# Graph layer with a mixture of experts on one core: ScalarE's 32 row transfers of each round go into the row buffer one round ahead, and one copy places all 128 rows

## The chip, the core and the metric

The kernel runs on one core of one Trainium2 chip. The metric is the device time of the whole program in microseconds (us), the median of several runs. A difference of about 0.2% is what a measurement of this kernel can tell from no change.

## The reference, cut to what matters

A graph of 6250 nodes with 256 features each and 200000 edges goes through one graph convolution, a mixture of 64 experts (two for each node), a normalisation over the nodes and a layer norm. The part that the change touches is the sum over the edges:

```python
deg_out = jnp.clip(jax.ops.segment_sum(ones, src, num_segments=n), 1.0)
deg_in = jnp.clip(jax.ops.segment_sum(ones, dst, num_segments=n), 1.0)
h = feats * jax.lax.rsqrt(deg_out)[:, None]
m = jax.ops.segment_sum(h[src], dst, num_segments=n) * jax.lax.rsqrt(deg_in)[:, None]
x = (m @ W_gc + b_gc) + (feats @ W_res + b_res)
```

`dst` is sorted, and it is drawn as 6250 * u**2. So the first nodes have many edges each and the last ones few: the kernel works on tiles of 128 nodes, and the first tile alone has a seventh of all edges, while the last tiles have some 2000 each.

## The kernel before, in words

First the kernel counts the edges of each source, scales the node features, and writes them to `table` in HBM. Then comes the edge stage, which is where the change lies. The edges stand in 1563 chunks of 128. Eight chunks make a group (1024 edges), six groups make a round: 196 groups, rounds 0 to 31 of six groups (q = 0 to 5), and a last round 32 of four. Group g is q = g % 6 of round g // 6. Each q has its own slot in a ring of six (`ring(q)`; slots 0 to 2 are shown as `ring`, slots 3 to 5 as `stage`).

- **GpSimd (POOL)** gathers a chunk with one indirect DMA (L516), 128 rows of 1 KB each. Before a group it waits for its indices (`idx_ready`) and until the slot is free (`acc_added`, L513). It takes all eight chunks of a group, but of the last slot (q = 5, `ROW_Q`) only seven. The eighth chunk of q = 5 comes row by row from two other queues, 128 single transfers of 1 KB for each of rounds 0 to 31.
- **SyncE (SP)** takes 96 of these rows. It loads the list of 128 sources (`list_rows`, L411, signal `listed`), reads the list into registers and issues 96 transfers into `row_buf`, which has two halves that alternate by round (L420). When they are there, it signals `rows_there` (L423). It works ahead: for round n it starts once round n - 2 was placed (`rows_placed`) and its list was read (`list_read`).
- **ScalarE (ACT)** takes the other 32 rows in four turns of eight (`fetch_rows`, L695), straight into the ring slot, after the steps q = 0 to 3 of the same round. Since it writes the slot itself, it first waits that the round before is added up (`acc_added >= it * RING`). After the fourth turn it copies SP's 96 rows from `row_buf` into the slot (`place_rows`, L702).
- In each step q ACT also writes the indices of the group six ahead (`indices`, L638), for which it waits that the group q of this round has been gathered, and then does its part of a **tick** if there is one.
- **VectorE (DVE)** makes a one-hot matrix for each group (L925; for group g it may start once the matmuls of group g - 2 are done, and it is next in line after the tick of the group before), a second one where a group reaches into another tile (L936), and adds the sums to `acc` (L1048).
- **TensorE (PE)** multiplies the one-hot matrices with the gathered rows (L1258, eight matmuls shown as x16). Before a group it waits for the gather, for the one-hot matrix, and for q = 5 also for `rows_placed` and for ACT's own 32 rows (`act_rows`).

A **tick** is the work on a tile of nodes that has all its edges: ACT copies the tile (L642, and L644 once the group is added), PE transposes and projects it, DVE adds and picks the experts, ACT writes the root (L665 to L671). It goes back and forth between the three engines. There are 49, one for each tile, and in the last rounds there is one for every second group.

After the last group POOL clears its buffers (L527, which waits for `acc_added` of all groups), and the expert stage follows: tables of slots, gathers, two matmuls for each of 64 experts, then the two normalisations.

Names: `step` is ACT's round, `ACT_TURNS` is 4, `SP_ROWS` 96, `par` the parity of the round. On ACT all rounds but 0 and 32 are one hardware loop.

Of the kernel before, what the change touches and what calls it, by code (L numbers as in the profile page):

```python
# [10 lines left out]
ACT = mybir.ActivationFunctionType  # L11
# [3 lines left out]
P = 128  # L15
N, D, EDGES = 6250, 256, 200000
# [8 lines left out]
CPG = 8  # L25
COLS = EB * P
GCOLS = COLS // CPG
RING = 6
HOTS = 2
GROUPS = -(-EDGES // (P * CPG))  # L30
STEPS = -(-GROUPS // RING)
# [6 lines left out]
ROW_Q = RING - 1  # L38
BLOCK = 32
SP_ROWS = 96  # L40
ACT_ROWS = 8
ACT_TURNS = (P - SP_ROWS) // ACT_ROWS
MAIN = 3
TG = 7
NB = NT // TG
# [17 lines left out]
def graph_moe_kernel(nc, x, src, dst, W_gc, b_gc, W_res, b_res, Wg, bg, w1, b1, w2, b2, gamma, beta, out):  # L63
    ctx = ExitStack()
    with ctx:
        def sb(name, shape, dt=F32):
            return ctx.enter_context(nc.sbuf_tensor(name, shape, dt))

        def sem(name):
            return ctx.enter_context(nc.semaphore(name))  # L70
# [55 lines left out]
        row_buf = sb("row_buf", [P, 2, D])  # L126
# [49 lines left out]
        def piece(n):  # L176
            taken_to[0] += n
            return arena[:, taken_to[0] - n:taken_to[0]]

        xg_pair = piece(2 * MAIN * D).rearrange("p (b k d) -> p b k d", b=2, k=MAIN)  # L180
        x30 = 4 * DK * H + 2 * D
        xg = [xg_pair[:, 0, :, :], xg_pair[:, 1, :, :],
              stage[:, x30:x30 + MAIN * D].rearrange("p (k d) -> p k d", k=MAIN)]
        AHEAD = len(xg)
        xgT = piece(MAIN * D).rearrange("p (k c r) -> p k c r", k=MAIN, c=DK)
        h1 = piece(MAIN * H).rearrange("p (k j r) -> p k j r", k=MAIN, j=HK)
        outs = piece(2 * MAIN * D).rearrange("p (b k d) -> p b k d", b=2, k=MAIN)
        xgx = piece(D)
# [40 lines left out]
        ha_ready, table_first, table_rest = sem("ha_ready"), sem("table_first"), sem("table_rest")  # L229
# [4 lines left out]
        rows_there, rows_placed, act_rows = sem("rows_there"), sem("rows_placed"), sem("act_rows")  # L234
        idx_ready = sem("idx_ready")
        gath = [sem(f"gath{q}") for q in range(RING)]
        hot_ready, group_mm, acc_added = sem("hot_ready"), sem("group_mm"), sem("acc_added")
# [12 lines left out]
        w1_in, w2_in, b2_in = ([sem(f"{w}_in{par}") for par in range(2)] for w in ("w1", "w2", "b2"))  # L250
        gathered = [[sem(f"gathered{b}{k}") for k in range(MAIN)] for b in range(AHEAD)]
        scattered = [[sem(f"scattered{par}{k}") for k in range(MAIN)] for par in range(2)]
# [31 lines left out]
        def ring(q):  # L284

            return ring_low[:, q, :, :] if q < RING // 2 else ring_high[:, q - RING // 2, :, :]

        def row_of(eng, reg):

            node = nc.s_assert_within(eng.snap(reg), 0, N - 1,  # L290
                                      skip_runtime_bounds_check_because="the list of sources holds nodes")
            return table[bass.ds(node, 1), :]
# [304 lines left out]
        def _(act):  # L597
# [82 lines left out]

            row_regs = [act.alloc_register(f"act_row{r}") for r in range(ACT_ROWS)]

            def fetch_rows(it, par, turn, first):
                r0 = SP_ROWS + turn * ACT_ROWS
                if turn == 0:
                    if first:
                        act.wait_ge(table_first, 16)
                        act.wait_ge(table_rest, 16 * (NB - 1))
                    else:
                        act.wait_ge(acc_added, it * RING)  # L690
                    act.wait_ge(listed, it * 16 + 16)
                    act.sem_inc(act_starts, 1)
                act.load(row_regs, row_list[0:1, bass.ds(par, 1), r0:r0 + ACT_ROWS])
                for r in range(ACT_ROWS):
                    act.dma_start(ring(ROW_Q)[r0 + r:r0 + r + 1, CPG - 1, 0:D], row_of(act, row_regs[r])).then_inc(act_rows, 16)  # L695
                if turn == ACT_TURNS - 1:
                    act.sem_inc(list_read, 1)

            def place_rows(it, par):
                act.wait_ge(rows_there, it + 1)  # L700
                act.sem_inc(act_starts, 1)
                act.activation(ring(ROW_Q)[0:SP_ROWS, CPG - 1, 0:D], row_buf[0:SP_ROWS, bass.ds(par, 1), :],  # L702
                               ACT.Copy).then_inc(rows_placed, 1)

            def step(it, first):
                par = 0 if first else nc.s_assert_within(act.snap(it & 1), 0, 1,
                                                         skip_runtime_bounds_check_because="it is a parity")
                for q in range(RING):
                    ahead = q + LEAD
                    indices(it + ahead // RING, ahead % RING, first and ahead < RING)  # L710
                    group_ticks(it * RING + q)
                    if q < ACT_TURNS:
                        fetch_rows(it, par, q, first)
                    if q == ACT_TURNS - 1:
                        place_rows(it, par)
            step(0, True)
            with act.Fori(1, STEPS - 1) as it:
                step(it, False)
            it = STEPS - 1
            for q in range(LASTQ):  # L720
                group_ticks(it * RING + q)
# [486 lines left out]
        def _(pe):  # L1208
# [114 lines left out]
            def step(it, first, final=False):  # L1323
                for q in range(LASTQ if final else RING):
                    g = it * RING + q
                    c = group_code(pe, g)
                    first_tile, last_tile = field(pe, c, 0), field(pe, c, 1)
                    n = LASTJ if final and q == LASTQ - 1 else CPG
                    pe.wait_ge(gath[q], it * (16 * pool_chunks(q, False)) + 16 * pool_chunks(q, final))
                    if q == ROW_Q and not final:  # L1330
                        pe.wait_ge(rows_placed, it + 1)
                        pe.wait_ge(act_rows, it * (16 * (P - SP_ROWS)) + 16 * (P - SP_ROWS))
                    if first and q == RING // 2:
                        pe.wait_ge(high_ones, 1)
                    pe.wait_ge(hot_ready, g + 1)
                    if not (first and q < 2):
                        pe.wait_ge(acc_added, g - 1)
                    multiply(banks[q % 2], hot[q % HOTS], q, group_mm, n)
                    with pe.If(last_tile > first_tile):
                        with pe.Fori(first_tile + 1, last_tile + 1) as t:  # L1340
                            pe.reg_add(extra, extra, 1)
                            seen = pe.snap(extra, min_val=1, max_val=GROUPS * NT)
                            pe.wait_ge(hotx_ready, seen)
                            multiply(banks[2], hotx, q, groupx_mm, n)
                    ticks_of_group(pe, c, tick)
            step(0, True)
            with pe.Fori(1, STEPS - 1) as it:
                step(it, False)
# [129 lines left out]
```

## Time and profile before

| what | value |
|---|---|
| median of 3 runs | 2916.74 us (2914.96 to 2917.04) |
| profiled execution, its own time | 2912.62 us |
| its span in the trace | 2910.8 us |
| mean granted TensorE clock | 0.833 |
| edge stage, first gather to last sum | 210 to 2162 us |
| PE busy | 2063.8 us (71%) |
| POOL busy | 1855.4 us (64%) |
| DVE busy | 1223.3 us (42%) |
| ACT busy | 444.0 us (15%) |

Times in the trace count from the start of the span. Register work, waits and the issue of DMAs are not counted as busy, so an engine with a small share can still be what another one waits for. A row of the timeline names the start, the duration, the engine and the line; in square brackets stands how long the engine was idle before it and what ended that. Where several things were waited for, the profile names the one that came last by its own reckoning.

### The profile page before, as it was taken

How to read it: one execution, taken by the hardware profiler on the slowest of the kernel's cores; microseconds unless marked ns; L12 is line 12 of the kernel's file. 1: busy time of each engine (PE TensorE's matmuls, PEld its weight loads, DVE VectorE, ACT ScalarE, POOL GpSimd, SP SyncE). 2: the span in 40 equal slices, each digit the busy share in tenths (PEclk: the TensorE clock that was granted, in tenths of full speed). 3: DMA queues.
4: the chain of work that ended last, by engine and by line, in shares of the span. 5: the costliest groups of instructions: out<-in, count | busy, mean ns of one | idle time of the engine just before them, and what ended most of it. 6: DMA issues, size and time to landing. Idle time of an engine off the chain costs nothing.

```text
span 2910.8 us, 57770 instructions
## 1 busy us (share of the span) xinstructions
PE 2063.8 (71%) x10204; PEld 1716.3 (59%) x10251; DVE 1223.3 (42%) x3115; ACT 444.0 (15%) x1390; POOL 1855.4 (64%) x1938
## 2 busy tenths in 40 slices
PE   8955556556666666767777768777766799999760
PEld 7954444445455555555556556565646788899650
DVE  8971112222323434344445455454553322222367
ACT  3010000000000101111111111111112223333213
POOL 0007777777777777777777777777715767777500
PEclk6557777888888878888988899998888999999885
DMA  8033333333333333333333333333314556666532
GB/s 301 0 99 109 109 108 107 108 110 109 109 109 110 112 109 110 111 111 111 113 111 113 112 113 113 112 115 112 112 31 139 168 166 204 198 197 202 188 113 88
DMA packets 211682, 361.84 MB, mean 124 GB/s; under 512 B 46696, under 2 KB 133558, under 8 KB 211534
## 3 DMA queue, kind: packets, MB, share of 16 engines
q0 software_dynamic: 92112, 226.49, 26.4%
q1 hardware_dynamic: 110266, 126.48, 13.5%
q10 hardware_dynamic: 9156, 7.48, 0.8%
q14 instruction: 127, 1.04, 0.1%
q8 instruction: 21, 0.34, 0.0%
HBM read 327.93 MB, written 57.52 MB: 132 GB/s over the span
## 4 chain that ended last, share of the span: by engine, by line
POOL 38%; PE 23%; issue 19%; DVE 9%; DMA 5%; DVEq 4%; ACTq 1%; POOLq 1%; ACT 1%; PEld 1%; SPq 0%; PEldq 0%
POOL ring L516 19%; POOL stage L516 18%; PE bank L1258 6%; PE bank L1379 6%; PE bank L1373 6%; PE bank L1238 3%; DMA y<-ring,slots 1%; DMA ring<-nodes,slots 1%; DMA stage<-y 1%; PE bank L1364 1%; DVE acc L1156 1%; DVE stage L839 1%; POOL y L551 1%; PEld bank L1448 1%; ACTq L695 1%
## 5 line engine op out<-in xcount | busy, mean ns | idle before, releaser
L516 POOL DMA_INDIRECT ring<-table,ring_idx x792 | 749.0, 946 | 242.1 <-issue 240.9
L516 POOL DMA_INDIRECT stage<-table,ring_idx x739 | 698.9, 946 | 225.1 <-issue 224.0
L1258 PE MATMUL bank<-stage 128*128 128x257 f32 x1030 | 323.1, 482 | 195.9 <-DMA stage<-table,ring_idx 87.1
L1258 PE MATMUL bank<-ring,hot 128*128 128x257 f32 x1056 | 316.1, 465 | 164.9 <-DMA ring<-table,ring_idx 119.2
L1258 PEld LDWEIGHTS bank<-stage 128*128 128x128 f32 x1030 | 249.9, 249 | 263.7 <-issue 132.4
L1258 PEld LDWEIGHTS bank<-ring,hot 128*128 128x128 f32 x1056 | 245.3, 238 | 229.5 <-issue 111.6
L1048 DVE TENSOR_TENSOR acc<-acc,bank 128x257 f32 x196 | 82.9, 423 | 491.1 <-PE bank L1258 464.2
L1373 PEld LDWEIGHTS bank<-ring,stage 128*128 128x128 f32 x1984 | 237.8, 197 | 9.7 <-issue 3.1
L1373 PE MATMUL bank<-ring,stage 128*128 128x128 f32 x1984 | 240.4, 281 | 2.4 <-DVE ring L1103 1.1
L1258 PE MATMUL bank<-ring,stage 128*128 128x257 f32 x528 | 170.6, 493 | 95.8 <-DMA ring<-table,ring_idx 70.7
L551 POOL DMA_INDIRECT y<-ring,slots x192 | 194.9, 1015 | 65.5 <-issue 48.6
L1379 PE MATMUL bank<-stage,ring 128*128 128x256 f32 x976 | 225.1, 384 | 8.8 <-ACT ring L737 7.3
L1258 PE MATMUL bank<-stage,hot 128*128 128x257 f32 x512 | 158.2, 476 | 91.5 <-DMA stage<-table,ring_idx 71.7
L1258 PEld LDWEIGHTS bank<-ring,stage 128*128 128x128 f32 x528 | 131.6, 256 | 132.3 <-issue 71.1
L1379 PEld LDWEIGHTS bank<-stage,ring 128*128 128x128 f32 x976 | 182.1, 192 | 34.1 <-issue 10.9
L1258 PEld LDWEIGHTS bank<-stage,hot 128*128 128x128 f32 x512 | 122.4, 245 | 124.9 <-issue 58.7
L737 ACT ACTIVATE ring<-bank,b1e 128x128 f32<-128x128 f32 x488 | 139.1, 368 | 356.3 <-PE bank L1373 356.3
L638 ACT ACTIVATE ring_idx<-srcT 128x8 int32 (+1 forms) x198 | 40.4, 206 | 930.2 <-DMA ring<-table,ring_idx 448.6
L541 POOL DMA_INDIRECT ring<-nodes,slots x129 | 137.3, 1064 | 67.7 <-issue 41.0
L1238 PE MATMUL bank<-stage 128*128 128x49 bf16 x1568 | 160.6, 279 | 6.6 <-DVE stage L839 5.7
L1238 PEld LDWEIGHTS bank<-stage 128*128 128x128 bf16 x1568 | 153.2, 150 | 14.1 <-DVE stage L839 13.6
L923 DVE TENSOR_SCALAR dstq<-dstT,neg_base 128x8 f32 (+1 forms) x196 | 48.7, 249 | 246.1 <-issue 240.8
(231 smaller groups left out, 2479.6 us busy)
## 6 DMA issues: line engine op xcount, KB each, us to landing
stage<-in_L_gnn_w_dram SPq DMA_DIRECT2D x128, 512.0 KB, 4.0
row_buf<-table SPq DMA_DIRECT2D x3072, 1.0 KB
stage<-table ACTq DMA_DIRECT2D x1024, 1.0 KB
ring<-table,ring_idx POOLq DMA_INDIRECT x792
y<-zeros SPq DMA_DIRECT2D x49, 256.0 KB, 2.4
stage<-y SPq DMA_DIRECT2D x14, 896.0 KB, 7.1
stage<-table,ring_idx POOLq DMA_INDIRECT x739
stage<-in_L_gnn_b_dram SPq DMA_DIRECT2D x64, 128.0 KB
```

Source lines behind the costliest of these rows:

```text
L516: pool.indirect_dma_start(out=ring(q)[:, j, 0:D], out_offset=None, in_=table[:, :], in_offset=bass.IndirectOffsetOnAxis(ap=ring_idx[:, q, ...
L541: pool.indirect_dma_start(out=xg[e % AHEAD][:, k, :], out_offset=None, in_=nodes[:, :], in_offset=bass.IndirectOffsetOnAxis(ap=gidx[:, col ...
L551: pool.indirect_dma_start(out=y2[:, :], out_offset=bass.IndirectOffsetOnAxis(ap=sidx[:, col:col + 1], axis=0), in_=outs[:, par, k, :], in_ ...
L638: act.activation(ring_idx[:, q, :], srcT[:, bass.ds((it * RING + q) * CPG, CPG)], ACT.Copy).then_inc(idx_ready, 1)
L695: act.dma_start(ring(ROW_Q)[r0 + r:r0 + r + 1, CPG - 1, 0:D], row_of(act, row_regs[r])).then_inc(act_rows, 16)
L737: last = act.activation(h1[:, k, j, :], banks[2 + k][:, j * P:(j + 1) * P], ACT.Gelu, bias=b1e[:, j:j + 1])
L923: dve.tensor_scalar(dstq[:, q, :], dstT[:, bass.ds(g * CPG, CPG)], neg_base[:, bass.ds(g, 1)], None, ALU.add)
L1048: dve.tensor_tensor(acc[:, bass.ds(first_tile, 1), :], acc[:, bass.ds(first_tile, 1), :], banks[q][:, 0:D + 1], ALU.add).then_inc(acc_adde ...
L1238: last = pe.matmul(banks[0][:, 0:HI], lo_hot[:, q, :, c], hi_hot[:, q, :, c], start=first and q == 0 and c == 0, stop=final and q == n - 1 ...
L1258: last = pe.matmul(bank[:, 0:D + 1], hots[:, j, :], ring(q)[:, j, :], start=j == 0, stop=j == n - 1)
L1373: last = pe.matmul(bank[:, j * P:(j + 1) * P], w1s[:, par, c, j * P:(j + 1) * P], xt[:, c, :], start=c == 0, stop=c == DK - 1)
L1379: last = pe.matmul(dst, h[:, j, :], w2s[:, par, j, :], start=j == 0, stop=j == HK - 1)
```

## The change

ACT's 32 rows now go into rows 96 to 127 of `row_buf`, in the half of the next round, and one copy places all 128 rows. The four turns for round it + 1 are issued after the steps q = 1 to 4 of round it; the copy for round it is made at q = 1, ahead of the first turn (in round 0 at q = 4). The rows of round 0 are fetched ahead of round 0, all four turns at once, and ACT waits for them. The wait for `acc_added` moves from the fetch to the copy, the wait for `act_rows` from PE to ACT. Round 31 fetches nothing and is written out behind the loop, which now has rounds 1 to 30.

```diff
+PLACE_Q = 1
...
-            def fetch_rows(it, par, turn, first):
+            def fetch_rows(it, par, turn):
                 r0 = SP_ROWS + turn * ACT_ROWS
                 if turn == 0:
-                    if first:
-                        act.wait_ge(table_first, 16)
-                        act.wait_ge(table_rest, 16 * (NB - 1))
-                    else:
-                        act.wait_ge(acc_added, it * RING)
                     act.wait_ge(listed, it * 16 + 16)
                     act.sem_inc(act_starts, 1)
                 act.load(row_regs, row_list[0:1, bass.ds(par, 1), r0:r0 + ACT_ROWS])
                 for r in range(ACT_ROWS):
-                    act.dma_start(ring(ROW_Q)[r0 + r:r0 + r + 1, CPG - 1, 0:D], row_of(act, row_regs[r])).then_inc(act_rows, 16)
+                    act.dma_start(row_buf[r0 + r:r0 + r + 1, bass.ds(par, 1), :], row_of(act, row_regs[r])).then_inc(act_rows, 16)
...
-            def place_rows(it, par):
+            def place_rows(it, par, first):
+                if not first:
+                    act.wait_ge(acc_added, it * RING)
+                    act.wait_ge(act_rows, it * (16 * (P - SP_ROWS)) + 16 * (P - SP_ROWS))
                 act.wait_ge(rows_there, it + 1)
                 act.sem_inc(act_starts, 1)
-                act.activation(ring(ROW_Q)[0:SP_ROWS, CPG - 1, 0:D], row_buf[0:SP_ROWS, bass.ds(par, 1), :],
-                               ACT.Copy).then_inc(rows_placed, 1)
+                act.activation(ring(ROW_Q)[:, CPG - 1, 0:D], row_buf[:, bass.ds(par, 1), :], ACT.Copy).then_inc(rows_placed, 1)
...
-                    if q < ACT_TURNS:
-                        fetch_rows(it, par, q, first)
-                    if q == ACT_TURNS - 1:
-                        place_rows(it, par)
+                    if q == (ROW_Q - 1 if first else PLACE_Q):
+                        place_rows(it, par, first)
+                    if rows and q > PLACE_Q - 1 and q - PLACE_Q < ACT_TURNS:
+                        fetch_rows(it + 1, other, q - PLACE_Q)
+            act.wait_ge(table_first, 16)
+            act.wait_ge(table_rest, 16 * (NB - 1))
+            for turn in range(ACT_TURNS):
+                fetch_rows(0, 0, turn)
+            act.wait_ge(act_rows, 16 * (P - SP_ROWS))
             step(0, True)
-            with act.Fori(1, STEPS - 1) as it:
+            with act.Fori(1, STEPS - 2) as it:
                 step(it, False)
+            step(STEPS - 2, False, False)
...
                         pe.wait_ge(rows_placed, it + 1)
-                        pe.wait_ge(act_rows, it * (16 * (P - SP_ROWS)) + 16 * (P - SP_ROWS))
```

## Rows read from the trace of the kernel before

**Rows 1.** The page: chain that ended last by engine, and the group of gathers.

```profile
POOL 38%; PE 23%; issue 19%; DVE 9%; DMA 5%; DVEq 4%; ACTq 1%; POOLq 1%; ACT 1%; PEld 1%; SPq 0%; PEldq 0%
...
L516 POOL DMA_INDIRECT ring<-table,ring_idx x792 | 749.0, 946 | 242.1 <-issue 240.9
```

**Rows 2.** Waits of POOL, whole span: us in total, times, longest us.

```profile
POOL ring L527 <- DVE acc L1048: 38.0, 1, 38.0
...
POOL ring L516 <- DVE acc L1048: 1.2, 4, 0.3
```

**Rows 3.** Chain in order of time, 1820 to 1892 us: start, us, what.

```profile
1835.63 3.02 DMA stage<-table,ring_idx
...
1838.89 8.89 PE bank L1258 x32
```

**Rows 4.** Waits of all engines, 1838.9 to 2161.7 us.

```profile
ACT mS L644 <- DVE acc L1048: 74.3, 12, 11.1
...
PE bank L1258 <- DMA stage<-table: 20.1, 3, 6.9
```

**Rows 5.** Timeline, a group that only its one-hot matrix held up (189).

```profile
2090.91 1.23 DVE L925 TENSOR_TENSOR stage<-bank,dstq 128x1024 f32<-128x1024 f32 x1
...
2092.19 5.42 PE L1258 MATMUL bank<-stage 128*128 128x257 f32 x16 [3.30 <-DVE stage L925]
```

**Rows 6.** Timeline around groups 167 (round 27) and 179 (round 29), q = 5.

```profile
1863.62 5.56 PE L1258 MATMUL bank<-stage 128*128 128x257 f32 x16 [6.66 <-DMA stage<-table]
...
1972.09 0.94 POOL L516 DMA_INDIRECT stage<-table,ring_idx  x1 [0.30 <-issue]
...
1973.62 1.22 DVE L925 TENSOR_TENSOR stage<-bank,dstq 128x1024 f32<-128x1024 f32 x1
...
1975.01 3.26 ACTq L695 DMA_DIRECT2D stage<-table  x8
...
1979.89 5.45 PE L1258 MATMUL bank<-stage 128*128 128x257 f32 x16 [5.51 <-DVE hot L925]
```

**Rows 7.** Timeline around group 185 (round 30, q = 5).

```profile
2043.73 1.22 DVE L925 TENSOR_TENSOR stage<-bank,dstq 128x1024 f32<-128x1024 f32 x1
...
2048.76 4.50 PE L1258 MATMUL bank<-stage 128*128 128x257 f32 x13 [6.90 <-DMA stage<-table]
```

**Rows 8.** Timeline around group 191 (round 31, q = 5).

```profile
2112.17 1.22 DVE L925 TENSOR_TENSOR stage<-bank,dstq 128x1024 f32<-128x1024 f32 x1
...
2116.80 5.27 PE L1258 MATMUL bank<-stage 128*128 128x257 f32 x16 [6.51 <-DMA stage<-table]
```

**Rows 9.** Chain of 1960 to 2020 us: the pass of group 181 on PE.

```profile
2001.26 10.20 PE bank L1258 x32
```

**Rows 10.** Lines of ACT's two copies: duration ns min/median/max, first and last start.

```profile
L702 ACT ACTIVATE stage<-row_buf x32: 417/417/418, 258.2 to 2115.6; 96x256 f32 x31, 96x256 f32<-96x256 f32 x1
...
L642 ACT ACTIVATE xS<-xs x49: 416/416/418, 498.2 to 2159.7; 128x256 f32 x49
```

**Rows 11.** Timeline, ACT between the ticks of groups 187 and 189.

```profile
2081.16 0.42 ACT L644 ACTIVATE mS<-acc 128x256 f32 x1 [5.99 <-DVE acc L1048]
...
2102.55 0.42 ACT L644 ACTIVATE mS<-acc 128x256 f32 x1 [1.29 <-DVE acc L1048]
```

**Rows 12.** Timeline, SP's rows of rounds 0 and 1, and group 5 on PE.

```profile
211.10 45.16 SPq L420 DMA_DIRECT2D row_buf<-table  x96
...
262.03 44.76 SPq L420 DMA_DIRECT2D row_buf<-table  x96
...
270.53 6.79 PE L1258 MATMUL bank<-stage 128*128 128x257 f32 x16 [3.36 <-DMA stage<-table,ring_idx]
```

**Rows 13.** Timeline, ACT in the round that is written out behind its loop.

```profile
2137.83 0.42 ACT L642 ACTIVATE xS<-xs 128x256 f32 x1 [2.12 <-issue]
...
2149.30 0.42 ACT L644 ACTIVATE mS<-acc 128x256 f32 x1 [11.06 <-DVE acc L1048]
```

**Rows 14.** Timeline, the same instruction of ACT inside the loop.

```profile
2074.76 0.42 ACT L642 ACTIVATE xS<-xs 128x256 f32 x1 [1.12 <-issue]
```

More of the change, by code:

```diff
@@ L694, in fetch_rows, with step @@
                 for r in range(ACT_ROWS):
-                    act.dma_start(ring(ROW_Q)[r0 + r:r0 + r + 1, CPG - 1, 0:D], row_of(act, row_regs[r])).then_inc(act_rows, 16)
+                    act.dma_start(row_buf[r0 + r:r0 + r + 1, bass.ds(par, 1), :], row_of(act, row_regs[r])).then_inc(act_rows, 16)
                 if turn == ACT_TURNS - 1:
                     act.sem_inc(list_read, 1)
-            def place_rows(it, par):
+            def place_rows(it, par, first):
+                if not first:
+                    act.wait_ge(acc_added, it * RING)
+                    act.wait_ge(act_rows, it * (16 * (P - SP_ROWS)) + 16 * (P - SP_ROWS))
                 act.wait_ge(rows_there, it + 1)
                 act.sem_inc(act_starts, 1)
-                act.activation(ring(ROW_Q)[0:SP_ROWS, CPG - 1, 0:D], row_buf[0:SP_ROWS, bass.ds(par, 1), :],
-                               ACT.Copy).then_inc(rows_placed, 1)
-            def step(it, first):
-                par = 0 if first else nc.s_assert_within(act.snap(it & 1), 0, 1,
-                                                         skip_runtime_bounds_check_because="it is a parity")
+                act.activation(ring(ROW_Q)[:, CPG - 1, 0:D], row_buf[:, bass.ds(par, 1), :], ACT.Copy).then_inc(rows_placed, 1)
+            def step(it, first, rows=True):
+                par, other = (0, 1) if first else [nc.s_assert_within(act.snap((it + a) & 1), 0, 1,
+                                                                      skip_runtime_bounds_check_because="it is a parity")
+                                                   for a in range(2)]
                 for q in range(RING):
```

## The prediction

> **What bounds the kernel now.** The page gives the outline: the chain that ended last runs 38% through POOL and 19% through issue [rows 1]. In the edge stage a gather takes 0.946 us and the next follows after 242.1 / 792 = 0.31 us [rows 1], a beat of 1.25 us, so 47 gathers set a round at 58.8 us. The waits of POOL say whether anything downstream slows that beat. They don't: for a free slot its gathers into `ring` waited 1.2 us in all, but once, behind the last gather, POOL stood 38.0 us until the last sum (L527) [rows 2]. So PE, DVE and ACT have fallen behind by then, and the end of the edge stage is theirs. Where does that begin? The chain in order of time leaves POOL for good at 1838.89, where PE starts on a gather issued at 1835.63 [rows 3]; from there to 2161.7 the ticks go round PE, DVE and ACT. What ends before 1838.89 is paid back by POOL's beat; what ends on the chain behind it counts in full.
>
> In that stretch PE waits 20.1 us in 3 waits for ACT's own rows [rows 4], all at q = 5: groups 167 (1863.62), 185 (2048.76) and 191 (2116.80) [rows 6 to 8]. Group 179 is a fourth under another name. Its wait ends at 1979.89 and is put down to a one-hot matrix, but its own matrix was ready at 1973.62 + 1.22 = 1974.84; ACT's rows were issued until 1975.01 + 3.26 = 1978.27 and a transfer has to land behind that [rows 6]. Nothing else that it waits for is due then.
>
> **The change, part by part.**
>
> *The rows' wait on PE goes.* The rows of a round are issued a round ahead, some 50 us before the copy, so PE's group q = 5 starts on the next latest of gather and one-hot matrix. Behind its matrix PE starts 2092.19 - (2090.91 + 1.23) = 0.05 us later [rows 5]. Behind a gather it starts 1838.89 - 1835.63 = 3.26 us after the last one was issued [rows 3].
> - Group 179: matrix 1974.84, and earlier if anything ahead of it is saved; gather 1972.09 + 3.26 = 1975.35. The gather decides, whatever group 167 saved before: 1979.89 - 1975.35 = **4.54 us**. Group 167's own saving is thus counted at nothing; POOL's beat takes it, and it would come back only if group 179 were not gather-bound.
> - Group 185: matrix 2043.73 + 1.22 + 0.05 = 2045.00, against 2048.76 [rows 7]: **3.76 us**.
> - Group 191: matrix 2112.17 + 1.22 + 0.05 = 2113.44, against 2116.80 [rows 8]: **3.36 us**.
>
> Together 11.66 us. POOL is far enough ahead to let them all through: from 1975.35 the gather of group 181 lands 16 beats later, at 1995.4, and PE takes it at 2001.26 [rows 9], 5.9 us in hand against 4.54; that of 185 lands a round later at 2034.1, 14.7 us in hand, that of 191 at 2092.9, 23.9 in hand. At the very end POOL has its 38.0 us.
>
> *What the matmuls do with it.* A pass of x32 that began behind a matrix took 10.20 us at group 181, one behind a longer wait 8.89 us [rows 3, 9]. A start behind a shorter wait may so cost between 0 and 1.3 us at each of three places, up to 3.9. I take 0.5 in all, since the first x16 took 5.42 us behind a matrix and 5.27 to 5.56 behind the rows [rows 5, 6, 8].
>
> *The copy.* 128 partitions instead of 96: the same width over 128 partitions takes 416 ns, over 96 it takes 417 [rows 10]. Nothing. It moves from the fourth step to q = 1, with the wait for `acc_added` and a new one for `act_rows`. Both are past: ACT has gone through the tick of the round before, and the rows are 50 us old.
>
> *The turns move by one step.* A turn is one load of registers and eight issues, 3.26 us in the timeline [rows 6], and the same 1024 transfers are issued in all. Behind ACT stand its ticks. At the tightest place, two turns between two ticks, ACT came to the copy of `acc` 1.29 us before it was released, of which the sum itself takes 0.42 [rows 11]: some 0.9 us in hand in a period of 21.39 us. For the pair q = 1 to q = 3 the copy comes on top of the two turns, 0.42 us and two waits: I estimate 0.6, inside 0.9. For q = 3 to q = 5 there are now two turns where there was one and the copy; the period was 24.7 and becomes 24.7 - 3.76 = 20.9, while ACT's own cycle is 21.39 - 0.9 = 20.5. It fits by 0.4. So nothing on the chain, but little in hand; the bounds are 0 and about 3 us over the five ticks of rounds 29 and 30. Round 31 has no turns at all.
>
> *The start.* ACT issues 32 rows before round 0, beside POOL's first gathers, and its indices for that round are already written. At q = 1 it then stands for the list of round 1, which SP loads after its 96 rows (211.10 + 45.16 = 256.3) [rows 12], so until about 260. Its turns follow and the copy is made at about 277, where PE would start group 5 at 270.53 [rows 12]: PE is 7 us late. In round 1 the copy needs SP's rows of round 1, issued until 262.03 + 44.76 = 306.8 and there by about 309, against a gather of q = 1 at about 291: 18 us. In round 2 it is 9 us, then SP is ahead, at 262.03 - 211.10 = 50.9 us a round [rows 12] against 58.8. POOL needs the indices behind these waits a round (58.8 us) later, and there is no tick yet. Nothing.
>
> **Sum:** 11.66 - 0.5 = 11.2 us off the profiled execution (2912.62 us), which lies 4.1 us below the median; off the median, 2916.74 - 11.2 = **2905.5 us**, 0.4% faster. The expert stage behind it starts from POOL's clearing and so moves as a whole.
>
> **The page on fetches.** In the round that is written out behind ACT's loop, the copy of the features came 2.12 us after the instruction before it, inside the loop 1.12 [rows 13, 14]: 1.0 us that a wait of 11.06 us covered. The Trainium skill, "Runtime: Kernel & Launch", section on instruction fetch mechanics, says that a taken branch whose target is outside the small window of fetched instructions stalls until it is fetched; the trace agrees in kind. The change writes a second round out in this way, 31, and that speaks against it: see the third rival.
>
> **The rivals.**
> 1. *ScalarE takes the row's place.* The turn after q = 4 and the copy before q = 3 make ACT late for the ticks. For it: 0.4 us in hand. Against it: outside the tightest pairs ACT waited 6.2 us on average (74.3 / 12) for the sums [rows 4]. If its cycle were 1 us longer than I reckon, five ticks lose 0.6 to 1 us each: 3 to 5 less, 2909.5 us.
> 2. *It doesn't do what it says.* The rows are early, but PE's wait stays, because the copy waits for SP's rows, or for something else at q = 1. For it: in rounds 1 and 2 it does. Against it: SP needs 50.9 of 58.8 us. Then 2916.7 us. The same comes out if the gain is spent before the expert stage.
> 3. *Unhidden fetches.* In round 31 ACT runs new instructions through three ticks; a stall of 1.0 us [rows 13, 14] inside each, where nothing covers it, gives 3 back: 2908.5 us.
> 4. *Slower.* SP and ACT are now coupled one round ahead through `listed`, `rows_placed` and `row_buf`. If SP's round, 45 us of issue and some 6 of waits, came above 58.8 us, SP would set the round in place of POOL. It would take over 7.8 us more, say from its transfers against ACT's in the same queues. At 60 us a round that is 1.2 x 31 = 37 us: 2954 us. The profile shows nothing near it.
>
> **How the numbers follow.** Forecast 0.66, rivals 0.13, 0.10, 0.07 and 0.04. The time is the forecast's. Its own bounds: up to 3.9 us of slower matmuls and 3 of ACT, less the 0.5 taken, say 2911 with both; downwards the 0.5, and the 2.1 us between the runs before: 2902. Rivals 1 and 3 lie inside; to 2912 the range leaves out rivals 2 and 4 and the tails, some 0.2. Within 0.2% means 2910.9 to 2922.6, about what a measurement of this kernel can tell from no change. Faster: the forecast, most of rivals 1 and 3: 0.81. Same: rival 2 and the upper tails: 0.15. Slower 0.04.
>
> **What would show it.** PE's waits for single rows are gone from the trace, and at q = 5 it starts on a gather or a matrix. POOL's beat stays 1.25 us and its last gather is issued at 2123.4 as before, but its wait at L527 falls from 38.0 to about 27 us. ACT's copy of `acc` still waits for the sum in rounds 29 to 31. In rounds 0 to 2 ACT stands at q = 1. I am wrong if POOL's wait stays near 38, if ACT's copy of `acc` starts at once behind the copy of the features in tick after tick (rival 1), or if POOL waits for indices or slots (rival 4).

## The result, and the profile after

The changed kernel took **2944.32 us** (median of 6 runs, 2939.99 to 2945.8) against 2916.89 us (6 runs, 2913.98 to 2925.9) for the kernel before on the same chip: ratio 1.0089, 95% interval 1.0075 to 1.0104. It is 0.9% slower where 0.4% faster was forecast. The profiled execution took 2945.8 us, its span is 2944.0.

The page of the kernel after: ScalarE's queue of transfers, the chain that ended last, and the first group of gathers. A queue row is packets, MB, share of 16 engines.

```profile
q10 hardware_dynamic: 37956, 7.54, 1.3%
...
POOL 29%; PE 24%; issue 18%; ACTq 10%; DVE 9%; DMA 5%; DVEq 3%; ACT 2%; PEld 1%; POOLq 1%; SPq 0%; PEldq 0%
...
L517 POOL DMA_INDIRECT ring<-table,ring_idx x792 | 749.6, 946 | 252.9 <-issue 240.3
```

The same queue on the page of the kernel before:

```profile
q10 hardware_dynamic: 9156, 7.48, 0.8%
```

Two things differ. ACTq, ScalarE's sequencer, had 1% of the chain [rows 1] and has 10%. And its queue moved 28,800 packets more for 0.06 MB more. ScalarE issues 1024 single rows; 960 of them, those issued in rounds 1 to 30, now go to a half of `row_buf` that a register chooses, and 960 x 30 = 28,800: **each of these rows leaves as 16 pieces of 64 bytes** in place of one of 1024. (Of the 30 packets more a row, 15 are the further pieces; that the other 15, of some 4 bytes each by the 0.06 MB, go one with each further piece is an inference.) The trace's field for the destination says it outright (an early row, whose half is a constant, and a later one; it reads [16,1] and 64 in 960 rows, [1,1] and 1024 in 64):

```
209.82   0.548  dst_num_elem=[1,1]  dst_elem_size=1024
1080.13  0.552  dst_num_elem=[16,1] dst_elem_size=64
```

(The first columns are start and duration in us. The first row's 0.548 us is another matter: it opens a turn, and in the kernel before, too, the first row of each turn takes 0.46 to 0.55 us and the other seven 0.23.)

What it costs the engine that issues stands in the view of one line. Kernel before, ScalarE's transfers, ns min/median/max:

```profile
L695 ACTq DMA_DIRECT2D stage<-table x1024: 223/232/550, 224.0 to 2115.0; - x171
```

Kernel after:

```profile
L691 ACTq DMA_DIRECT2D row_buf<-table x1024: 226/552/676, 209.8 to 2090.6; - x171
```

0.552 us in place of 0.232. A turn, from its load of registers to the end of its eighth issue, takes 6.60 us (median over 128 turns) in place of 3.96: 2.6 us more, four times a round.

This makes ScalarE late. The timeline of ScalarE, kernel after, around the tick of group 179, which answers to [rows 11]:

```profile
1996.29 5.84 ACTq L691 DMA_DIRECT2D row_buf<-table  x8
...
2004.22 5.94 ACTq L691 DMA_DIRECT2D row_buf<-table  x8
2010.31 0.21 ACT L639 ACTIVATE ring_idx<-srcT 128x8 int32 x1 [7.82 <-issue]
2012.21 5.82 ACTq L691 DMA_DIRECT2D row_buf<-table  x8
2018.34 0.21 ACT L639 ACTIVATE ring_idx<-srcT 128x8 int32 x1 [7.83 <-issue]
2019.41 0.42 ACT L643 ACTIVATE xS<-xs 128x256 f32 x1 [0.86 <-issue]
2019.73 0.40 ACT L645 ACTIVATE mS<-acc 128x256 f32 x1
```

and PE at the same place:

```profile
2020.19 0.69 PE L1280 MATMUL bank<-ident,mS 128*128 128x128 f32 x2 [9.37 <-ACT mS L645]
```

In [rows 11] the copy of `acc` stood 5.99 and 1.29 us for the sum. Here it follows the copy of the features with no wait at all. The tick before this one was that of group 176, so three turns of 6.6 us stand between the two, where the kernel before had two of 4.0 us and the copy; the sum was ready at 2011.20, and PE stands 9.37 us. Over the span 16 of the 49 copies of `acc` come without a wait for the sum, all from group 118 on, where 4 did in the kernel before. The waits of PE tell of the whole span (us in total, times, longest). Kernel before:

```profile
PE bank L1258 <- DMA stage<-table: 60.3, 11, 7.0
PE bank L1275 <- ACT mS L644: 52.7, 49, 2.0
```

Kernel after:

```profile
PE bank L1280 <- ACT mS L645: 118.2, 48, 9.4
```

The wait for single rows is gone, as meant. The wait for ScalarE's copy has more than doubled, and its longest is 9.4 us where 2.0 was. The waits of the last stretch, 1838.9 to 2192.6 us, against [rows 4]:

```profile
ACT mS L645 <- DVE acc L1053: 61.1, 9, 11.5
...
PE bank L1280 <- ACT mS L645: 40.3, 15, 9.4
...
POOL ring L517 <- ACT ring_idx L639: 6.8, 3, 6.2
POOL stage L517 <- ACT ring_idx L639: 6.4, 3, 5.8
POOL ring L517 <- DVE acc L1053: 4.5, 3, 3.9
```

POOL has 17.7 us of waits here that it did not have: ScalarE's indices and, as PE falls back, the slots of its ring. Its last gather is issued at 2140.60 where it was at 2123.37. POOL's waits, whole span, against [rows 2]:

```profile
POOL ring L528 <- DVE acc L1053: 51.6, 1, 51.6
```

Between the last gather and the last sum lie 51.6 us in place of 38.0. 17.2 + 13.6 = **30.8 us**: the last sum comes at 2192.6 us in place of 2161.7. The span grew by 33.2; the stages behind took 2.3 more.

On PE this is only in part time that it stands. The stretch from the sum of group 117 to the last sum, with the same groups in each, in the kernel before, in the kernel after, and in e17 of the experiments below, which has the changed order and whole transfers:

```profile
core 0: us, PE busy (x) PEld busy (x) DVE busy (x) ACT busy (x) POOL busy (x), PEclk, DMA share, GB/s
1377.00:2162.10 785.10, 585.23 (x2451) 464.78 (x2482) 392.81 (x1318) 123.99 (x399) 565.34 (x598) 0.90 0.37 108
```

```profile
1377.40:2193.00 815.60, 609.35 (x2450) 481.90 (x2482) 394.26 (x1317) 122.30 (x398) 565.91 (x598) 0.87 0.37 104
```

```profile
1377.70:2149.10 771.40, 586.19 (x2449) 467.03 (x2481) 392.62 (x1317) 124.73 (x398) 566.71 (x599) 0.90 0.38 110
```

The stretch is 30.5 us longer than before, and PE is busy 24.1 us longer in it with the same matmuls, at a mean granted clock (PEclk, a mean of its two levels, 1.2 and 2.4 GHz) of 0.87 in place of 0.90. The stands themselves grew by only 6.4 us, as the rows' waits that went are set against them; held against e17 the stretch is 44.2 us longer, 23.2 busy and 21.0 standing. So about half of what the late copies cost PE shows as slower matmuls. Between e14 and e15 below it is 15.4 of 40.8 us, again with 0.87 and 0.90. That the clock is lower because PE stands longer for the copies fits all of these, but no run tests it by itself.

Where no row is fetched any more, the forecast's picture holds. Timeline of PE, kernel after, groups 185 and 191, against [rows 7, 8]:

```profile
2078.75 5.43 PE L1263 MATMUL bank<-stage 128*128 128x257 f32 x16 [2.25 <-DVE stage L930]
...
2147.72 5.25 PE L1263 MATMUL bank<-stage 128*128 128x257 f32 x16 [3.07 <-DVE stage L930]
```

Both start on the one-hot matrix. In round 31, which has no turns, two groups take 20.9 to 21.3 us from sum to sum, as forecast; in the kernel before the two up to group 191 took 24.5.

### The profile page after: what moved, and what is told of

It reads as the page before. It is cut to its first block, busy times and chain, and to the rows that moved or that the text cites. A ratio compares the mean times of both kernels' runs of the same rounds, so it can differ in the third digit from the quotient of the medians.

```text
span 2944.0 us, 57804 instructions
## 1 busy us (share of the span) xinstructions
PE 2084.1 (71%) x10204; PEld 1728.0 (59%) x10251; DVE 1225.5 (42%) x3115; ACT 444.2 (15%) x1390; POOL 1856.1 (63%) x1938
## 3 DMA queue, kind: packets, MB, share of 16 engines
q0 software_dynamic: 92112, 226.49, 26.5%
## 4 chain that ended last, share of the span: by engine, by line
POOL 29%; PE 24%; issue 18%; ACTq 10%; DVE 9%; DMA 5%; DVEq 3%; ACT 2%; PEld 1%; POOLq 1%; SPq 0%; PEldq 0%
POOL ring L517 14%; POOL stage L517 13%; ACTq L691 7%; PE bank L1383 6%; PE bank L1377 6%; PE bank L1263 5%; PE bank L1243 3%; PE bank L1301 2%; DMA y<-ring,slots 2%; DMA stage<-y 1%; DMA ring<-nodes,slots 1%; PE bank L1368 1%; ACTq L689 1%; ACTq L291 1%; DVE stage L844 1%
## 5 line engine op out<-in xcount | busy, mean ns | idle before, releaser
L1263 PE MATMUL bank<-ring,hot 128*128 128x257 f32 x1056 | 322.6, 472 | 176.6 <-DMA ring<-table,ring_idx 132.1
L1263 PE MATMUL bank<-stage 128*128 128x257 f32 x1030 | 307.2, 463 | 152.4 <-DMA stage<-table,ring_idx 82.8
L1263 PEld LDWEIGHTS bank<-stage 128*128 128x128 f32 x1030 | 238.3, 237 | 215.6 <-issue 80.5
L1377 PEld LDWEIGHTS bank<-ring,stage 128*128 128x128 f32 x1984 | 237.0, 196 | 10.8 <-issue 4.6
L1263 PE MATMUL bank<-ring,stage 128*128 128x257 f32 x528 | 163.3, 477 | 81.9 <-DMA ring<-table,ring_idx 63.7
L1263 PEld LDWEIGHTS bank<-ring,stage 128*128 128x128 f32 x528 | 126.5, 245 | 116.0 <-issue 58.5
```

Of the source, the lines that this page charges most:

```text
L1263: last = pe.matmul(bank[:, 0:D + 1], hots[:, j, :], ring(q)[:, j, :], start=j == 0, stop=j == n - 1)
L1377: last = pe.matmul(bank[:, j * P:(j + 1) * P], w1s[:, par, c, j * P:(j + 1) * P], xt[:, c, :], start=c == 0, stop=c == DK - 1)
```

## The experiments

T1 is the theory that the cut transfers are the loss and the order itself (rows a round ahead, one copy) a gain; T1a that their price is ScalarE's time, T1b that it is the packets. T2 is that the order is the loss. What tells T1 from T2 is a kernel with the order changed and the transfers whole. For that the half of the buffer has to be a constant of the program, so ScalarE's loop of rounds is written as one of two rounds:

```diff
-                    act.dma_start(row_buf[r0 + r:r0 + r + 1, bass.ds(par, 1), :], ...
+                    act.dma_start(row_buf[r0 + r:r0 + r + 1, par, :], ...
-            with act.Fori(1, STEPS - 2) as it:
-                step(it, False)
+            with act.Fori(0, (STEPS - 3) // 2) as i:
+                for a in range(2):
+                    step(i * 2 + (1 + a), (1 + a) % 2, False)
```

(the same in the load of the registers and in the copy). "Version with whole transfers" below means this. The form of the loop is so changed with it, and was not tested alone; a turn takes 3.95 us in e17 and 3.96 in the kernel before, so the form makes no turn shorter than it was.

**First: runs on other ground.** The first eleven runs, five sets on five chips, fell where the kernel before itself took 4238 to 4297 us and not 2917. Each is held against the kernel before of its own set. What was different there shows in SyncE's transfers, L420. Kernel before:

```profile
L420 SPq DMA_DIRECT2D row_buf<-table x3072: 224/225/311, 211.1 to 2026.7; - x192
```

Run e3, the same program there, with one stretch of SyncE's timeline:

```profile
L420 SPq DMA_DIRECT2D row_buf<-table x3072: 1/225/1393, 211.4 to 3294.1; - x192
```

```profile
1999.43 77.30 SPq L420 DMA_DIRECT2D row_buf<-table  x92
```

The median is the same, but in stretches register moves, other register work and issues take some 0.70 us each, up to 1.4. There are some 1200 such steps on SyncE up to the last gather and some 650 on ScalarE, and 5 in all in the profile of the kernel before. From first to last issue SyncE's 96 rows take 88.8 us (median) in place of 44.6, and a round follows every 96 us: there SyncE sets the round, not POOL. Why the sequencers step so slowly there is not known. These runs answer their own question only in part:

e1 and e5, the version with whole transfers:

> The changed kernel with one thing undone: the half of row_buf is a constant of the program instead of a run-time offset (ACT's loop holds two rounds, 1 to 30 in 15 turns), so that each row transfer is one piece of 1 KB again and not 16 of 64 B. Order of turns and copy as in the change. Theory 1 (the issue of a cut transfer, 0.55 us instead of 0.23, makes ACT late for the ticks): a turn falls from 6.7 to about 4.0 us, PE's waits for ACT's copy of acc (L1280 in the changed kernel, 118 us) fall back to about 53, POOL's wait behind its last gather to about 27 us, and the time is what was forecast blind, 2903 to 2908 us, 0.4% below the kernel before. Theory 2 (the new order of turns and copy makes ACT late): 2935 to 2945 us still. Theory 3 (the 28800 additional packets slow the queues): also 2903 to 2908, so this run doesn't tell 1 from 3.

> The kernel of e1_static once more, on a chip where the kernel before runs at about 2917 us as in the first comparison (in the first set it took 4238 us, the issue of transfers bound it, and SP and not POOL set the rounds). Theory 1 (price of the cut transfers on ACT): a turn of 4.0 us, PE's waits for ACT's copy of acc near 53 us, POOL's wait behind its last gather near 27, time 2903 to 2908 us. Theory 2 (order of turns and copy): 2935 to 2945 us.

Measured 4273.48 and 4270.8 us, ratios 1.0077 (1.0056 to 1.0098) and 1.0066 (1.0047 to 1.0085). Neither theory's number, as neither reckoned with SyncE's round.

e2, e1 with register moves ahead of each row:

> As e1_static, and ahead of each of ACT's row transfers five register moves, some 0.35 us in all (0.07 each), so that a turn takes about 6.8 us as in the changed kernel, with whole transfers in the queue. Theory 1 (ACT's time): 2940 to 2950 us, as the changed kernel. Theory 3 (packets): as e1_static, about 2905. Theory 2: as e1_static, whatever that gives.

Ratio 1.0083 (1.0057 to 1.0109), but a turn's issues took 3.26 us (median) as in e1: the moves made no pause. It tells nothing apart.

e3, the kernel before with an index meant to be a register's; it became a constant and the transfers stayed whole:

> The kernel before with one thing added: the chunk of the ring slot that ACT's rows go to is given as a run-time offset (its value is always 7), so that each row transfer is cut into 16 pieces; direct into the slot, turns at q = 0 to 3 and PE's wait for the rows as before. Theory 1: a turn takes 6.7 us, the ticks come late and PE's wait for the rows grows by 2.7 us at each q = 5 that counts: slower by 25 to 45 us, 2942 to 2962. Theory 2 (order): 2915 to 2919, as before. Theory 3: also slower, by as much as the changed kernel, 2944.

4238.85 us, ratio 1.0000 (0.9986 to 1.0014). A null run, and a measure of the ground.

e4, e1 with the copy and the turns one slot earlier (`PLACE_Q = 0`):

> As e1_static with PLACE_Q = 0: the copy at q = 0 and the turns for the next round behind q = 0 to 3. If ACT's order matters (theory 2), this differs from e1_static by over 5 us; if only the price of an issue does (theory 1), it lies within 2 us of it, at about 2905: the pair of ticks at q = 3 and 5 then has one turn less between it, the pair 5 and 1 one turn and the copy more.

4288.1 us, ratio 1.0106 (1.0086 to 1.0125): 0.3% or 15 us behind e1. By its own rule (over 5 us) this spoke for the order; as SyncE sets the round there, it says nothing of the ground of the prediction, and e19 below puts the question again there.

e7, the kernel before in its own order, with its rows cut:

```diff
+            last_chunk = act.alloc_register("act_last_chunk")
+            act.reg_mov(last_chunk, CPG - 1)
-                    act.dma_start(ring(ROW_Q)[r0 + r:r0 + r + 1, CPG - 1, 0:D], ...
+                    act.dma_start(ring(ROW_Q)[r0 + r:r0 + r + 1, bass.ds(chunk, 1), 0:D], ...
```

> The kernel before with one thing added: the chunk of the ring slot that ACT's rows go to comes from a register (always 7), and with a destination whose address is known only at run time each row transfer leaves the program as 16 pieces of 64 B. (In e3_before_cut the offset had been folded to a constant and the transfers had stayed whole: that kernel is the kernel before.) Turns at q = 0 to 3, direct into the slot, PE's wait as before. Theory 1 (ACT's time for the issue of a cut transfer, 0.55 us against 0.23): a turn takes 6.7 us instead of 4.0, ticks and rows come late: 25 to 45 us slower than the kernel before of the same set, where POOL sets the rounds. Theory 2 (the order of turns and copy): no slower than it. Theory 3 (packets): slower by the 27 us of the change.

4384.51 us against 4296.51, ratio 1.0204 (1.0177 to 1.0232). Its queue moved 39,876 packets, and its issues:

```profile
L700 ACTq DMA_DIRECT2D stage<-table x1024: 3/552/1526, 227.3 to 3424.5; - x171
```

**An index in a register cuts the transfer in the old order as in the new**, at 552 ns again, and it costs 2.0% (88 us) there with nothing else changed.

e8 and e9, the changed kernel and the version with whole transfers side by side:

> The changed kernel itself, unaltered, on the same chip as the version with whole transfers (its neighbour in this call, e9). T1 (cut transfers make ScalarE late): where the kernel before takes 2917 us, 2944 us again; where it takes 4240 to 4300 us, this kernel is 1.5% or more behind the version with whole transfers, since cutting alone cost the kernel before 2.0% there (e7). T2 (the order by itself, a round ahead and one copy, makes it slow): this kernel and the version with whole transfers take the same time within 0.3%.

> The changed kernel with the half of the buffer a constant of the program, so that ScalarE's transfers stay whole, timed beside the changed kernel itself. T1: 2903 to 2908 us where the kernel before takes 2917; where the kernel before takes 4240 to 4300 us, 0.7% behind it as in e1 and e5, and 1.5% or more ahead of the changed kernel of e8. T2: the changed kernel's time within 0.3%.

4471.73 and 4341.28 us against 4296.64: ratios 1.0421 (1.0382 to 1.0459) and 1.011 (1.008 to 1.014). The cut costs 130 us there, so T2 falls as the main cause. The loss of the order itself, 0.7% to 1.1%, is real on this ground.

e10, e11 and e12. e10 is the version with whole transfers and ScalarE's time put back without the packets:

```diff
+        idle = sb("idle", [P, D])
                 act.load(row_regs, row_list[0:1, par, r0:r0 + ACT_ROWS])
+                for n in range(5):
+                    act.drain()
+                    act.activation(idle[:, :], xs[:, n, :], ACT.Copy)
```

e11 has the turns in slots 0 to 3 and the copy in slot 3 (`PLACE_Q = 3`); e12 is the version with whole transfers again.

> Transfers whole as in e1, but five copies of 128x256 that nobody reads, each with a drain ahead, stand ahead of every turn's issues: about 5 x (0.42 + 0.07) = 2.4 us more of ScalarE a turn, without a packet more (the cut transfers add 2.7 us a turn). T1a (ScalarE's time is what costs, not the packets): where the kernel before takes 2917 us, 2937 to 2947; where it takes 4240 to 4300 us, 2% to 3% above the version with whole transfers (e12), as the changed kernel was in e8 against e9. T1b (the 28800 packets are what costs): within 0.3% of e12 in either case.

> Transfers whole, the turns in slots 0 to 3 as before and the copy of all rows in slot 3 as before, in place of both from slot 1 on. If what is left of the loss of the version with whole transfers where the kernel before takes 4240 to 4300 us (0.7% to 1.1%) is ScalarE's stand in slot 1 for SP's rows, this takes the kernel before's time or up to 0.5% less there; if it is ScalarE's turns or anything else of the order, it stays 0.7% to 1.1% behind. Where the kernel before takes 2917 us: 2903 to 2908.

> The version with whole transfers once more, as the neighbour of e10 and e11 on one chip. Where the kernel before takes 2917 us: 2903 to 2908; where it takes 4240 to 4300 us: 0.7% to 1.1% behind the kernel before, as in e1, e5 and e9.

4300.53, 4323.49 and 4341.89 us, ratios 1.0015 (0.9999 to 1.003), 1.006 (1.004 to 1.0081) and 1.0099 (1.0077 to 1.012). e10 fits neither T1a nor T1b: with more of ScalarE's time it is 1% faster than e12. Its rounds on SyncE come every 95.9 us (median), e12's every 97.3; why is open. By e10, ScalarE's time is no price where SyncE sets the round. In e8 SyncE's rounds come every 101.2 us on average, in e9 every 97.6, and 31 x 3.6 = 112 us is most of the 130 measured: there the cut shows as a longer round of SyncE. e11 gains 0.4% on e12 and stays 0.6% behind the kernel before, so neither of its cases holds. ScalarE's stand for SyncE's rows went with it, by the waits of e12

```profile
ACT stage L701 <- SPq L424: 644.7, 26, 52.2
```

and of e11

```profile
ACT stage L700 <- SPq L424: 66.3, 1, 66.3
```

but half of the loss stayed, so that stand explains a part of it at most.

**SyncE's round taken out of the way.** In e13 to e16 SyncE fetches 12 of each 32 rows; the other 60 of its 96 hold zeros, set once at the start. These kernels leave out a part of the sums, and what they send to the experts differs, so they are held against each other and not against the kernel before.

```diff
+SHORT = 12
-                    for r in range(BLOCK):
+                    for r in range(SHORT):
-                    sp.wait_ge(sp_rows[b], it * (16 * BLOCK) + 16 * BLOCK)
+                    sp.wait_ge(sp_rows[b], it * (16 * SHORT) + 16 * SHORT)
```

> The kernel before, but SyncE fetches 12 of each 32 rows of its list; the other 60 of its 96 rows hold zeros, set once at the start. The base of the next three. Where the kernel before takes 2917 us: within 0.2% of it, as SyncE's round does not set anything there. Where it takes 4240 to 4300 us: if SyncE's round sets the round there, some 31 x (96 - 70) = 800 us less; if not, the same.

> The changed kernel with the same 36 rows on SyncE (the other 60 hold zeros). T1a (ScalarE's time costs) and T1b (packets cost) alike: 0.9% or more above e13, and 1% to 1.5% above e15. T2 (the order costs): within 0.3% of e15.

> The version with whole transfers, with the same 36 rows on SyncE (the other 60 hold zeros). T1a and T1b: 0.3% to 0.5% below e13 (ScalarE no longer stands between PE and its own rows). T2: 0.9% above e13.

> As e15, with five copies of 128x256 that nobody reads ahead of each turn's issues (2.4 us more of ScalarE a turn, no packet more; the other 60 rows hold zeros). T1a (ScalarE's time costs): within 0.3% of e14. T1b (the packets cost): within 0.3% of e15.

These fell where the kernel before takes 2921.34 us: 2906.46, 2929.49, 2889.16 and 2917.36 us, ratios 0.9951 (0.9932 to 0.9969), 1.0029 (1.0012 to 1.0046), 0.9893 (0.9874 to 0.9911) and 0.9989 (0.9977 to 1.0001). The order alone, with its loop of two rounds, gains 17.3 us (e15 against e13), the cut costs 40.3 (e14 against e15), and ScalarE's time alone 28.2 (e16 against e15). T2 falls. T1a is right in kind; its "within 0.3% of e14" missed by 0.1%. Three more expectations were narrowly missed: e13 was to be within 0.2% of the kernel before and is 0.5% faster; e14 was to be 0.9% or more above e13 and is 0.8%; e15 was to be at most 0.5% below e13 and is 0.6%. POOL's wait behind its last gather ranks e14, e16 and e15 in the same order (e16's profile is of the fastest of its ten executions, 2906.91 us). e14:

```profile
POOL ring L532 <- DVE acc L1057: 51.6, 1, 51.6
```

e16:

```profile
POOL ring L533 <- DVE acc L1060: 41.4, 1, 41.4
```

e15:

```profile
POOL ring L532 <- DVE acc L1056: 24.9, 1, 24.9
```

**The whole kernels, on the ground of the prediction.** e17 is the version with whole transfers, e18 that of e10, e19 that of e11.

> The version with whole transfers, all rows fetched. Where the kernel before takes 2917 to 2921 us: T1 (the cut transfers are the loss, the order itself gains) 0.3% to 0.6% below the kernel before, 2900 to 2910 us; T2 (the order is the loss) 0.7% or more above it.

> As e17 with five unread copies of 128x256 ahead of each turn (2.4 us more of ScalarE a turn, no packet more), where the kernel before takes 2917 to 2921 us. T1a (ScalarE's time costs most of it): 25 to 35 us above e17, near the changed kernel's 2944. T1b (packets cost): within 0.3% of e17.

> Whole transfers, turns in slots 0 to 3 and the copy in slot 3, as the kernel before has them, but fetched a round ahead. Where the kernel before takes 2917 to 2921 us, the place of the turns makes no difference if only their length counts: within 0.2% of e17.

Against 2919.42 us for the kernel before:

| run | what | us | ratio (95%) |
|---|---|---|---|
| e17 | whole transfers | 2904.13 | 0.9956 (0.9941 to 0.9972) |
| e18 | and five copies a turn | 2931.51 | 1.0039 (1.0024 to 1.0054) |
| e19 | old slots | 2904.28 | 0.9955 (0.9938 to 0.9971) |

Undoing the cut, with the loop of two rounds that this takes, turns 0.9% slower into 0.4% faster: e17 beats both kernels. The place of the turns makes no difference (e19). The page of e17, ScalarE's queue:

```profile
q10 hardware_dynamic: 9156, 7.48, 0.8%
```

its transfers, and its waits of PE and POOL:

```profile
L691 ACTq DMA_DIRECT2D row_buf<-table x1024: 217/225/552, 210.3 to 2045.2; - x171
```

```profile
PE bank L1279 <- ACT mS L645: 51.3, 48, 1.9
```

```profile
POOL ring L528 <- DVE acc L1052: 22.4, 1, 22.4
```

PE waits for ScalarE's copy as before (51.3 against 52.7 us), and POOL's wait is down from 38.0 [rows 2] to 22.4. e18 lays 2.0 us a turn on it (5.98 us from the load to the last issue, against 3.95) and not one packet of data. Its timeline of ScalarE behind group 179, to be held against the one of the kernel after:

```profile
1997.62 2.35 ACT L693 ACTIVATE idle<-xs 128x256 f32<-128x256 f32 x5 [1.97 <-issue]
1999.71 3.24 ACTq L695 DMA_DIRECT2D row_buf<-table  x8
2003.26 0.21 ACT L640 ACTIVATE ring_idx<-srcT 128x8 int32 x1 [3.29 <-issue]
2004.52 0.42 ACT L644 ACTIVATE xS<-xs 128x256 f32 x1 [1.05 <-issue]
2004.84 0.40 ACT L646 ACTIVATE mS<-acc 128x256 f32 x1
```

Again the copy of `acc` comes without a wait (17 of the 49 do, 2 in e17). PE's and POOL's waits follow:

```profile
PE bank L1283 <- ACT mS L646: 92.4, 48, 8.1
```

```profile
POOL ring L529 <- DVE acc L1056: 50.0, 1, 50.0
```

ScalarE's time by itself, 2.0 us a turn, costs 27.4 us. By the same rate the 2.6 us of the cut transfers would be 27.4 x 2.65 / 2.03 = 36 us, an estimate that takes the price as linear. The cut costs 1.0089 - 0.9956 = 1.3%, 39 us. So 27 of the 39 us are shown to be ScalarE's time, and by the estimate nearly all of them are. That the price is linear was not tested: e16 lies 12 us below e14, as e18 lies 13 below the kernel after, and whether the packets have a part in these 12 us stays open. They don't show in the gathers that run beside them. POOL's queue, kernel after and e17:

```profile
q0 software_dynamic: 92112, 226.49, 26.5%
```

```profile
q0 software_dynamic: 92112, 226.49, 26.9%
```

26.5% of 2944.0 us and 26.9% of 2898.8 are both 780 us: the same packets took the same time with and without the 28,800 others.

## Why the prediction was wrong

- **The step that failed** is the one headed *The turns move by one step*: "A turn is one load of registers and eight issues, 3.26 us in the timeline, and the same 1024 transfers are issued in all", put at "nothing on the chain", bounds 0 and about 3 us. The number of transfers is the same, but the operation is not: its destination moved from an address that the program fixes to one that a register gives. The eight issues take 5.84 us, not 3.26. The row used for the price was of another form of the instruction, and the diff showed that: `bass.ds(par, 1)` in the destination. SyncE's rows, which go to the same buffer, have a constant half (L420) and were no measure either. With 2.6 us a turn in the place of 0, the step's own text gives the sign: two turns between two ticks are 5.2 us more against "0.4 us in hand". For the ticks of groups 183 and 185, two turns each, the copy of `acc` came 3.2 and 3.9 us after the sum; for that of 179, behind three turns, 8.5 (in e17, with the same three turns whole, 1.1).
- *What the matmuls do with it*, put at 0 to 3.9 us, looked only at how a pass begins. The 24.1 us that PE was busy longer at the lower mean clock were in no term. (In *How the numbers follow*, the upper bound with both adds up to 2911.9, not "say 2911"; nothing hangs on it.)
- *The pieces.* The Trainium skill, "DMA: Bandwidth & Descriptors", in the paragraph on how many engines under "Why a DMA increments its semaphore by 16 and not by 1", says that a transfer is shared by the largest number of engines up to 16 that divides the outer size of its access patterns, and that software can split a contiguous `[1, N]` pattern "so that it sprays". The trace agrees in kind: 16 pieces of 64 bytes, 28,800 packets more. What the pieces add to an issue, 0.32 us, is read from the rows here.
- **11.66 us for the rows' wait** was right. It is gone in the kernel after. In e17 the sums of groups 179, 185 and 191 come 4.2, 9.0 and 12.3 us earlier than in the kernel before, against 4.5, 8.3 and 11.7 by the forecast's terms, and the last sum comes at 2148.6 us in place of 2161.7: 13.1 us earlier, against 11.2 forecast. The time of e17, 15.3 us below the kernel before with an interval of 8 to 17, bears the sum out. But e17 is another program: the forecast's 2905.5 us is near its time, not that of the kernel that was forecast.
- **The copy** over 128 partitions takes 0.42 us as reckoned.
- **The start** was right in kind. ScalarE, kernel after, in rounds 0 and 1:

```profile
276.37 0.42 ACT L701 ACTIVATE stage<-row_buf 128x256 f32<-128x256 f32 x1 [1.13 <-issue]
...
310.86 0.42 ACT L701 ACTIVATE stage<-row_buf 128x256 f32 x1 [20.09 <-SPq L424]
```

  The copy was put at "about 277" and the rows at "about 309". In the kernel after PE starts group 5 at 276.89; in e17 the same stands cost nothing that its total shows.
- **Rival 1**, ScalarE takes the row's place, had the mechanism and 3 to 5 us for it. With two turns between two ticks its cycle was not 1 us longer but 5, the copy of `acc` came late from group 118 on, and the price was some 40 us. It should have had a case of its own that ends slower than before. The sign that the prediction set for it, ACT's copy of `acc` at once behind the copy of the features in tick after tick, is what the trace shows.
- **Rival 2** fell: in the kernel after, PE waits for no single row.
- **Rival 3** fell. ScalarE in round 31, written out, kernel after, against 2.12 [rows 13] and 1.12 [rows 14]:

```profile
2105.60 0.42 ACT L643 ACTIVATE xS<-xs 128x256 f32 x1 [0.78 <-issue]
...
2126.51 0.42 ACT L643 ACTIVATE xS<-xs 128x256 f32 x1 [0.76 <-issue]
```

  The two copies in round 32 still come after 1.67 and 1.91 us. The 2.12 of the kernel before is of that round too, so the longer wait belongs to round 32 and not to a round's being written out. The stall at taken branches that the prediction cites from the Trainium skill (the page is titled "Runtime: NRT & Kernel Launch") is thus not seen in these rows, though the prediction says that they agree in kind.

- **Rival 4**, the slower one, was another mechanism: SyncE's round at over 58.8 us. It did not happen on the ground of the prediction (a round of SyncE takes 46.4 us from first to last issue, against 44.6; its rows and ScalarE's go by queues of their own, q1 and q10 on the page). Where the kernel before takes 4240 to 4297 us SyncE sets the round in both kernels, and there the order alone is 0.7% to 1.1% slower.

## What to carry to other kernels

When an edit lets a register choose where a DMA lands, price it as a new instruction: look at the queue's packets for the same bytes and at the duration of one issue, before and after. Often the register is only a parity, and a loop written over two rounds makes it a constant again. An engine that issues transfers between its compute steps is as late as its issues are long, whatever the transfers themselves hide behind.

## What the runs showed of the hardware that was not expected

- The same 1024-byte row took 0.23 us of ScalarE's sequencer to issue as one piece and 0.55 us as 16. With ScalarE's rows cut, SyncE's own issues, whole as before, went from a median of 225 to 238 ns.
- The kernel before took 2917 to 2921 us in some sets of runs and 4238 to 4297 us in others, with sequencer steps of 0.70 us in stretches. Ratios of two kernels do not carry over from one to the other: the version with whole transfers is 0.4% faster on the first ground and 0.7% to 1.1% slower on the second.
- With 60 of SyncE's 96 rows a round left out, the kernel before was 0.5% faster (e13: 2906.46 against 2921.34 us). Of the 13.9 us between the two profiles' spans (2910.8 and 2896.9 us), 11.5 lie behind the last sum, where the zeros change what the experts are sent; so this is no measure of what SyncE's rows cost the edge stage.
